# Attention results carried by transfers instead of transposes, in a transformer layer for one core

## The reference, cut to what matters

```python
x = x + _layernorm(attn(_layernorm(x)))       # attn below, z = _layernorm(x)
zn = _layernorm(z) * ln_scale + ln_bias
q, k, v = heads(zn @ w_qkv)                   # 16 heads, 16 columns each
scores = einsum('bhqd,bhkd->bhqk', q, k) / 4
att = softmax(scores, axis=-1)
out = einsum('bhal,bhlv->bhav', att, v)       # heads side by side: 1024 x 256
attn = z + out @ w_proj + b_proj
x = x + _layernorm(ffn(_layernorm(x)))        # gated shared part, 8 experts on 512 rows
```

## Time and profile before

| what | value |
|---|---|
| median of 3 runs | 1044.52 us (1044.05 to 1045.02) |
| profiled execution, its time | 1043.87 us |
| its span, first to last instruction | 1042.1 us |
| PE busy | 959.6 us, 92% |
| DVE busy | 813.2 us, 78% |
| ACT busy | 626.6 us, 60% |
| POOL busy | 333.7 us, 32% |
| mean granted TensorE clock | 0.968 |

### The profile page before, as it was taken

How to read it: one execution, slowest core, us unless ns; L and a number is a source line. 1 busy time by engine, 2 the same in 40 slices (tenths; PEclk the granted TensorE clock), 3 DMA queues, 4 the chain that set the end, 5 groups by cost and what they waited for, 6 DMA issues and landing times.

```text
span 1042.1 us, 16606 instructions
## 1 busy us (share of the span) xinstructions
PE 959.6 (92%) x6370; PEld 388.0 (37%) x6372; DVE 813.2 (78%) x1595; ACT 626.6 (60%) x736; POOL 333.7 (32%) x457
## 2 busy tenths in 40 slices
PE   4289999999999999999999999999999999965985
PEld 3132333333334334333343344333432433235773
DVE  4187888998877987989869878889699788335765
ACT  3024677777875776777767776767676767831110
POOL 4061003001633261216915422227352022633022
PEclk9696999999999999999999999999999999997998
DMA  5905101330151113200631022102511000231001
GB/s 138 138 1 69 54 2 42 50 72 4 40 86 39 42 42 46 70 9 1 106 98 42 1 34 56 36 2 60 86 59 42 1 1 2 69 139 57 1 1 61
DMA packets 45783, 49.42 MB, mean 47 GB/s; under 512 B 8408, under 2 KB 38888, under 8 KB 45320
## 3 DMA queue, kind: packets, MB, share of 16 engines
q1 hardware_dynamic: 44360, 46.53, 20.2%
q10 hardware_dynamic: 960, 0.79, 0.7%
q0 software_dynamic: 384, 1.05, 0.3%
HBM read 13.94 MB, written 8.91 MB: 22 GB/s over the span
## 4 chain that ended last, share of the span: by engine, by line
PE 84%; DVE 9%; ACT 2%; DMA 2%; issue 2%; POOL 1%; SPq 0%; ACTq 0%; DVEq 0%; POOLq 0%
PE obank L949 23%; PE sc L935 20%; PE ring L917 16%; PE ring L832 10%; PE ring L854 5%; DVE mx L1163 4%; PE sc L1024 3%; PE ring L824 3%; PE ring L975 2%; DVE st L1099 1%; ACT prob L760 1%; DMA kp<-parts 1%; PE ring L969 1%; DMA x_sb<-x 0%; DMA qp<-mp 0%
## 5 line engine op out<-in xcount | busy, mean ns | idle before, releaser
L1163 DVE TENSOR_REDUCE mx<-ring 128x1 f32<-128x512 f32 x1024 | 635.4, 682 | 134.9 <-PE ring L917 133.5
L760 ACT ACTIVATE prob<-sc 128x1024 f32<-128x1024 f32 x512 | 495.9, 1021 | 129.9 <-PE sc L935 128.6
L935 PE MATMUL sc<-qp,kp 48*128 48x512 bf16 (+1 forms) x2048 | 274.8, 379 | 1.3 <-DMA qp<-mp 0.5
L917 PE MATMUL ring<-kp,qp 48*128 48x512 bf16 x1024 | 247.5, 390 | 30.2 <-issue 20.7
L949 PE MATMUL obank<-prob,vaug 128*32 128x512 f32 x2048 | 274.5, 608 | 0.7 <-ACT prob L760 0.7
L917 PEld LDWEIGHTS ring<-kp,qp 48*128 48x128 bf16 x1024 | 75.1, 93 | 260.4 <-DVE mx L1163 155.8
L935 PEld LDWEIGHTS sc<-qp,kp 48*128 48x128 bf16 (+1 forms) x2048 | 99.4, 95 | 104.4 <-ACT prob L760 19.2
L543 POOL TENSOR_TENSOR hid<-hid,b 128x512 f32<-128x512 f32 x24 | 30.6, 1275 | 150.3 <-ACT hid L725 150.3
L551 POOL TENSOR_TENSOR resid<-qkf,parts 128x1024 f32<-128x1024 f32 x11 | 23.5, 2135 | 171.1 <-ACT parts L697 171.1
L949 PEld LDWEIGHTS obank<-prob,vaug 128*32 128x32 f32 x2048 | 40.3, 108 | 64.4 <-issue 61.7
L557 POOL TENSOR_SCALAR parts<-resid 128x1024 bf16<-128x1024 f32 x14 | 14.7, 1050 | 120.0 <-DVE resid L1153 119.0
(11 more groups left out here) (194 smaller groups left out, 845.7 us busy)
## 6 DMA issues: line engine op xcount, KB each, us to landing
kp<-parts SPq DMA_DIRECT2D x96, 128.0 KB, 5.0
qp<-parts SPq DMA_DIRECT2D x180, 64.0 KB, 2.6
x_sb<-x SPq DMA_DIRECT2D x7, 1024.0 KB, 5.6
out<-hid SPq DMA_DIRECT2D x4, 1024.0 KB, 4.6
x_scratch<-x SPq DMA_DIRECT2D x3, 1024.0 KB, 4.8
qp<-mp SPq DMA_DIRECT2D x128, 2.0 KB
kp<-ew SPq DMA_DIRECT2D x1, 2048.0 KB, 7.7
x_sb<-x SPq DMA_DIRECT2D x2, 512.0 KB, 4.5
```

The source lines that it names most:

```text
L760: nc.scalar.activation(prob[:, e % 2, 2 * a:2 * a + 2, :].rearrange("p g n -> p (g n)"), sbuf2[a][:, :], ACT.Exp, scale=0.25).then_inc(s_f ...
L917: nc.tensor.matmul(dst[:, :], qp[rows, qh, h, qt * P:(qt + 1) * P], kp[rows, h, kh * HALF:(kh + 1) * HALF], start=True, stop=True).then_in ...
L935: ins = nc.tensor.matmul(dst[:, j * HALF:(j + 1) * HALF], kp[rows, h, kt * P:(kt + 1) * P], qp[rows, qh, h, :], start=plane == 0, stop=pla ...
L1163: nc.vector.tensor_reduce(mx[:, u % 2, n:n + 1], src[:, :], AX.X, ALU.max).then_inc(rv_free, 1)
```

## The change

- `ot` and `a` are gone, with `anat`. SP carries each unit's results from `oT` to `yA`, head by head (four transfers of 16 rows), which lies as the projection wants it.
- SP spreads the four rows of 512 sums over 128 partitions, 16 each (`total`); DVE takes their reciprocals (`reciprocals`); SP writes these to DRAM and reads them back, each row onto the 16 partitions of its head (`sums`). Seven transfers a unit in all. POOL multiplies `yA` by `sums` for two units at a time (`over_sums`, at tau 43, 51, and 14, 19 of the next batch).
- The last unit has no time for this: its sums go to `sums` directly by one broadcast transfer, two of its four result transfers are issued by ACT, and DVE takes reciprocals and product itself in two halves (`last_results`).
- `mt` moves to the begin of slots tau 2, 10, 17, 25, 33, 41, 57, and 48 (there behind the fill). 2 and 10 are the same place for PE as the ends of 1 and 9.
- The transposes `z` of the next batch move from tau 10 to 13 to tau 14 to 17.
- The selector rows `pick` are made at the end of the loop instead of at the start, in the place of other data.

```diff
-Z_AT = (14, 10)
+Z_AT = (14, 14)
+MT_AT = (2, 10, 17, 25, 33, 41, 48, 57)
+MT_LATE = 48
+D_AT = (43, 51, 14, 19)
+ROWS = 16 * (1 + GH)
...
-        if 1 <= w < B and 15 <= tau < 19:
-            fill.append(("a", w - 1, tau - 15))
...
+        mt = [("mt", t // 8 - 1)] if tau in MT_AT and 0 <= t // 8 - 1 < B * HU else []
+        row = fill + mt if tau == MT_LATE else mt + fill
...
-        if e >= 0 and e % 8 == 2 and 0 <= e // 8 - 1 < B * HU:
-            row.append(("ot", e // 8 - 1))
...
+            def result_rows(u):
+
+                b, g, qh = u // HU, u % HU // NH, u % NH
+                row, cols = GH * HD * (g % 2), slice(qh * HALF, (qh + 1) * HALF)
+                sp.wait_ge(s_oT, u + 1)
+                if u < B * HU - 1:
+                    if u >= NH:
+                        sp.wait_ge(s_recip, u - 1)
+                    sp.dma_start(total[:, qh, :], oT[HD:P:VW, qh, :]).then_inc(s_total[qh], 16)
+                else:
+                    sp.dma_start(sums[row:row + GH * HD, qh, :], oT[HD:P:VW, qh, :].rearrange("p (o n) -> p o n", o=1)
+                                 .to_broadcast([GH, HD, HALF])).then_inc(s_rows[qh], 16)
+                if u % HU == 0 and b > 0:
+                    sp.wait_ge(r_full, R_INDEX["p", b - 1, 3] + 1)
+                for i in range(GH if u < B * HU - 1 else GH // 2):
+                    sp.dma_start(yA[row + i * HD:row + (i + 1) * HD, g // 2, cols],
+                                 oT[i * VW:i * VW + HD, qh, :]).then_inc(s_rows[qh], 16)
...
+                for u in range(B * HU):
+                    first = 8 * u + 8 + LEAD + (4 if u % HU == 0 else 1)
+                    if t == first:
+                        result_rows(u)
+                    if t == first + 3 and u < B * HU - 1:
+                        reciprocals_out(u)
+                    if t == first + 4 and u < B * HU - 1:
+                        reciprocals_in(u)
...
+            def over_sums(b, kk, qh):
+                u = HU * b + (2 * kk + 1) * NH + qh
+                cols = slice(qh * HALF, (qh + 1) * HALF)
+                pool.wait_ge(s_rows[qh], ROWS * (u // NH + 1))
+                nc.gpsimd.tensor_tensor(yA[:, kk, cols], yA[:, kk, cols], sums[:, qh, :], ALU.mult).then_inc(s_div, 1)
...
                 elif kind == "p":
-                    if key[2] == 0:
-                        pe.wait_ge(ra_free, TAKEN["a", b, 2 if b == B - 1 else 3][1] + 1)
-                    if key[2] == 2 and b == B - 1:
-                        pe.wait_ge(ra_free, TAKEN["a", b, 3][1] + 1)
-                    project(key, yT, key[2], wp, KD)
+                    if key[2] % 2 == 0:
+                        pe.wait_ge(s_div, 4 * b + 3 + key[2] // 2)
+                    elif key[2] == 3 and b == B - 1:
+                        pe.wait_ge(s_div, 4 * b + 5)
+                    project(key, yA, key[2], wp, KD)
...
+            def reciprocals(u):
+                qh = u % NH
+                ve.wait_ge(s_total[qh], 16 * (u // NH + 1))
+                if u >= NH:
+                    ve.wait_ge(s_over[qh], 16 * (u // NH))
+                nc.vector.reciprocal(over[:, qh, :], total[:, qh, :]).then_inc(s_recip, 1)
...
+                for u in range(B * HU - 1):
+                    if t == 8 * u + 8 + LEAD + (6 if u % HU == 0 else 3):
+                        reciprocals(u)
...
             for i in range(4):
                 h = i // 2
+                if i == 1:
+                    last_results(0)
+                    last_results(1)
```

More of the change, by code:

```diff
@@ L78, in ring_order @@
             fill.append(("w", w - 1, tau - 59))
-        row = fill
+        mt = [("mt", t // 8 - 1)] if tau in MT_AT and 0 <= t // 8 - 1 < B * HU else []
+        row = fill + mt if tau == MT_LATE else mt + fill
         if t < NS:
             row += [("max", t, j) for j in range(4)]
-        if t % 8 == 1 and 0 <= t // 8 - 1 < B * HU:
-            row.append(("mt", t // 8 - 1))
-        if e >= 0 and e % 8 == 2 and 0 <= e // 8 - 1 < B * HU:
-            row.append(("ot", e // 8 - 1))
         at[t] = row
     last = B - 1
-    at[SLOTS] = ([("a", last, i) for i in HALVES] + [("p", last, i) for i in range(4)]
+    at[SLOTS] = ([("p", last, i) for i in range(4)]
                  + [("x", last, 0), ("x", last, 2), ("h", last, 0), ("h", last, 1), ("x", last, 1), ("x", last, 3)]
@@ L155, in build @@
         hid = sb("hid", [P, NT, D])
-        anat = sb("anat", [P, NT, D])
+        yA = sb("yA", [P, KD, N])
+        sums = sb("sums", [P, NH, HALF])
+        total = sb("total", [P, NH, GH * HALF // P])
+        over = sb("over", [P, NH, GH * HALF // P])
         act = sb("act", [P, NT, F])
@@ L196, in build @@
         lv = {k: sb("lv_" + k, [P, NT]) for k in LN}
-        neg = {k: sb("neg_" + k, [P, B if k == "z" else 1, NT]) for k in LN}
+        neg = {k: sb("neg_" + k, [P, B if k == "z" else 1, NT]) for k in LN[:5]}
         rstd = {k: sb("rstd_" + k, [P, B if k == "z" else 1, NT]) for k in LN}
@@ L219, in build @@
         pickb = resid[:, HALF:N].bitcast(bf16).rearrange("p (e n) -> p e n", e=E)
-        xg, xgn = anat[:, 0:MT, :], anat[:, MT:2 * MT, :]
+        xg, xgn = (yA[:, i, :].rearrange("p (t d) -> p t d", d=D) for i in range(2))
+        pick = qkf[0:E, :].rearrange("p (e n) -> p e n", e=E)
         mhid = x_sb[:, 0:MT, :]
@@ L364, in pack_step, with reciprocals_out, reciprocals_in @@
                                      parts[src, 1, q, qh * HALF:(qh + 1) * HALF]).then_inc(s_pack[1], 16)
+            def result_rows(u):
[14 more added lines that the diff above has]
+                                 oT[i * VW:i * VW + HD, qh, :]).then_inc(s_rows[qh], 16)
+            def reciprocals_out(u):
+                sp.wait_ge(s_recip, u + 1)
+                sp.dma_start(over_dram[u, :].rearrange("(p n) -> p n", p=P), over[:, u % NH, :]).then_inc(s_over[u % NH], 16)
+            def reciprocals_in(u):
+                b, g, qh = u // HU, u % HU // NH, u % NH
+                n = 4 * b + 2 * (g // 2) + qh
+                row = GH * HD * (g % 2)
+                sp.wait_ge(s_over[qh], 16 * (u // NH + 1))
+                if g % 2 == 0 and n >= 2:
+                    sp.wait_ge(s_div, n - 1)
+                sp.dma_start(sums[row:row + GH * HD, qh, :],
+                             over_dram[u, :].rearrange("(i o n) -> i o n", i=GH, o=1).to_broadcast([GH, HD, HALF]))\
+                  .then_inc(s_rows[qh], 16)
             sp.dma_start(x_sb[:, 0:4, :], x_tiles[0, :, 0:4, :]).then_inc(s_xhalf, 16)
@@ L400, in _ @@
                 w, tau = divmod(t, SL)
-                if t % 8 == 1 and 0 <= t // 8 - 1 < B * HU:
+                if tau in MT_AT and 0 <= t // 8 - 1 < B * HU:
                     u = t // 8 - 1
@@ L597, in _ @@
                     z_with_bias(w - 1)
+                if tau in D_AT:
+                    kk, qh = divmod(D_AT.index(tau), NH)
+                    if 0 <= w - kk and w - kk < B and (w, qh) != (B, 1):
+                        over_sums(w - kk, kk, qh)
                 if 1 <= w < B and tau - 1 in P_AT:
@@ L771, in _ @@
             last = B - 1
+            u = B * HU - 1
+            sc.wait_ge(s_oT, u + 1)
+            for i in range(GH // 2, GH):
+                nc.scalar.dma_start(yA[GH * HD + i * HD:GH * HD + (i + 1) * HD, KD - 1, HALF:N],
+                                    oT[i * VW:i * VW + HD, u % 2, :]).then_inc(s_rows[1], 16)
             for key in RING_AT[SLOTS]:
-                if key[0] in ("a", "x"):
+                if key[0] == "x":
                     ring_item(key)
@@ L953, in _ @@
                 for key in RING_AT[t]:
-                    if key[0] not in ("max", "mt", "ot"):
+                    if key[0] == "mt":
+                        u = key[1]
+                        dst = open_r("mt", u)
+                        pe.wait_ge(s_nm, u + 1)
+                        nc.tensor.transpose(dst[0:GH * QT, 0:P], nm[:, u % 2, :], ident[:, :]).then_inc(r_full, 1)
+                    elif key[0] not in ("max", "ot"):
                         ring_item(key)
@@ L964, in _ @@
                     value_product(e - 1)
[L965 to L976 removed]
             last = B - 1
             for key in RING_AT[SLOTS]:
[L980 removed]
+                if key[0] in ("p", "x") or key[0] == "h" and key[2] < 3:
                     ring_item(key)
@@ L1245, in _ @@
                 w, tau = divmod(t, SL)
+                mt = [key for key in RING_AT[t] if key[0] == "mt"]
+                if mt and tau != MT_LATE:
+                    ring_item(mt[0])
                 if tau in (2, 3) and w + 1 < B:
@@ L1290, in _ @@
                 for key in RING_AT[t]:
-                    if not by_act(key):
+                    if not by_act(key) and (key[0] != "mt" or tau == MT_LATE):
                         ring_item(key)
@@ L1357, in _ @@
             src = take_r("oh")
+            ve.wait_ge(s_clear, 1)
             nc.vector.tensor_copy(ohTb[0:E, :], src[0:E, 0:M]).then_inc(rv_free, 1)
```

95 lines of the change are left out of this document (32 added, 63 removed).

## The result

| | before | after |
|---|---|---|
| median of 4 runs each | 1044.28 us (1042.98 to 1045.02) | 1030.33 us (1028.27 to 1033.38) |
| ratio, 95% interval | | 0.9873 (0.9858 to 0.9888) |
| profiled execution, its time | 1043.87 us | 1030.68 us |
| its span | 1042.1 us | 1028.9 us |
| mean granted TensorE clock | 0.968 | 0.958 |

What follows compares the result with a forecast made beforehand. PE, busy 92% of the span, was taken as the bound. From 1043.87 us, 30.6 saved up to the last value product and 16.3 paid back at the end, plus 0.65 for the median, gave 1030.2; 8-in-10 range 1019 to 1041.

Steps and rivals of the forecast that it cites:

- ot: Removed `ot` transposes: 21 plain slots at 0.90 us, -19.0; six before a fill, -2.3; one in the tail, -0.5.
- a and tau 14: Removed `a` transposes: tau 14, with `ot`, 2.05 us three times, -6.2; nine other `a` at 0.58, -5.2.
- The new reciprocals: 31 added reciprocals on DVE, 0.2 us each in about 25 plain slots: +5, between 0 and 9.
- mt: Moved transposes of the maxima: seven get a fill behind them, 0.42 us each; together -3.4, between 0 and -5.
- Waits for the spread sums: DVE waiting for the transfer of sums before its reciprocals: +1 us for three batches, up to 4.
- Rival (2): Spread sums land too late in every unit, stopping DVE and PE: slower than before, 1055 if landing at 5.5; chance 0.08.
- The reload: Last batch's reload of x, now behind the last result transfers, delays `z_with_bias` and DVE's first addition: +11.2 us.
- The last results: Two reciprocals of 256 elements and two products on DVE behind the first addition: +4.4 us, between 1.6 and 5.5.
- The cold clock: After PE's idle time before the third projection, two projections may run at 1.2 GHz: +0.7 us, 0 to 3.
- Rival (1): The end isn't late: the reload does not hold the additions, or PE's last projections end late anyway; 1019, chance 0.1.
- Rival (3): DVE, not PE, bounds plain slots: `ot` gives 0.42 instead of 0.70 in 21 units, `mt` nothing; 1039.6, chance 0.15.
- Rival (4): A new wait on SP delays stacked keys or rows of maxima, 3 to 5 us per batch: 1042, chance 0.07.

Runs made afterwards that it cites:

- e5: The changed kernel with each of the 31 spread reciprocals done twice on DVE: 1033.71 us, 0.9896 of the kernel before.
- e3: The changed kernel with the `mt` transposes back at the ends of slots 8u+9: 1033.43 us, 0.9892 of the kernel before.
- e6: The changed kernel with the transfer that spreads the sums issued behind its unit's four result transfers: 1037.86 us, 0.9934 of the kernel before.
- e1: The changed kernel with the last batch's reload of x issued at slot 260, ahead of the last results: 1017.74 us, 0.9741 of the kernel before.
- e4: The kernel before the change, with the last batch's reload of x held until the last copy to `oT`: 1055.32 us, ratio 1.0108.
- e9: The changed kernel with reload at slot 260, last `z_with_bias` earlier on POOL, `last_results` behind DVE's second addition: 1015.85 us, 0.9723 of the kernel before.

## Why the prediction was right, and where it was not

1.1 us lie between the spans' predicted and measured difference (14.3 and 13.2), but much more than that cancelled. The two mechanisms, a shorter PE and a late reload, were right; that the time came out within 0.2 us of the forecast is luck.

- **Reading slot by slot.** That a slot is read as 2.49 and what it has more led to -30.6 up to the last result; -31.1 was measured.
- **ot.** Right. Slots at tau 22 and 46 are shorter by 0.39, as said, and the plain ones by 0.88 with the new reciprocal in them.
- **a and tau 14.** Right in the mechanism, 2 us too large. Tau 14 is shorter by 1.46 to 1.53 (-2.05 with 0.58 of `z` put there in two batches and a waiting reciprocal in the last), tau 9 to 18 together by 2.7, 3.7 and 3.1 in the second, third and last batch. 11.4, and about 0.5 for the moves of `mt` there, was forecast, 9.6 is the sum; 1.0 of the gap is the wait for a row of maxima at tau 12 of the second batch.
- **The new reciprocals: the step that failed most.** I took 0.2 of their 0.26 in 25 slots, +5, since a slot with `nm` had 0.12 more. They cost 0.02 each. e5 shows why: only a second one in the same place costs, and that 0.11. The extra 0.12 of `nm` did not mean that DVE's slack was gone.
- **mt.** I took -3.4. Against e3, the slots that a moved `mt` touches give 0.6 us. The 3.4 that e3's profile has in four slots come once each, and e3's 2.0 by ratio lie within the intervals. Of the seven places that I priced at 0.42 each, tau 57 gave 0.18, and tau 24 of the last batch took back what tau 25 gave, 0.51. What failed most was "as dear as at 49" for tau 48: behind `nm` and two gate products it costs 0.67 where 0.42 was saved, and 1.0 in the first batch. I had the reciprocals 4.5 us too dear, `mt` nearly 3 and `a` some 2 too good, and so the sum came out right.
- **Waits for the spread sums.** +1, and 0.4 was measured. Rival (2) did not occur; e6 shows that it was some 2 us of queue away.
- **The reload.** Mechanism and place right, shown by e1 and e4. The size was 2.4 short: the transfers ahead took 3.33 us (890.61 to 893.94) instead of 1.9, since the last of them took SP 2.04 and not 0.64, and the reload took 6.76 to POOL's first use instead of 5.8. `z_with_bias` took 8.9, as said.
- **The last results.** +4.4, and 4.1 measured. The slope from two small reciprocals gave 1.8 for 256 elements; 1.75 was measured. (0.08 / 12 is 6.7 ns and not 6.5, which would have given 1.9.) The page-based estimate, the Trainium skill's ("VectorE: DVE Perf Modes", section "First, the fixed hardware budget") repeat count of 8, gave 2.1 and a fixed part on top, and is too dear: 1.75 us over 256 elements is 6.8 ns each with all fixed parts in.
- **The cold clock.** +0.7 was put on the path. The third and fourth projections did run slower, 6.08 us for their 16 matmuls where the first two take 3.72, at a clock of 0.60 (window below), but DVE was busy 6.36 of the 6.60 us beside them, so nothing was added to the path. In e9, where DVE has less to do there, 1.46 us are.

```profile
913.00:919.60 6.60, 6.08 (x16) 4.63 (x16) 6.36 (x16) 0.00 (x0) 1.22 (x2) 0.60 0.01 2
```

Rival (1) is what e1 turned the kernel into, 0.9741 or 1017 us, where the prediction put it at 1019. Rival (3) falls with the plain slots, 0.88 shorter and not 0.42, and e5 agrees. Rival (4) has one trace: the 0.91 us at 278.85.

## What to carry to other kernels

When transfers that wait for late results are put into an in-order queue, look at what stands behind them: here a prefetch that had been hidden for 20 us lost its cover and took back 14 of 31 us, and its old place in the queue gave them back. Price an engine's added work by its slack in the slot, not by its duration: the first 0.24 us in a slot of 2.49 was free, the second cost half. And a sum of terms that comes out right is no proof of the terms; two of mine were off by about 3 and 5 us with opposite signs, and only slot lengths read one by one told that.
